# Other positions for projections, convolutions and C in the background of a chunk, and another position for the first shifted copies

## The reference

```
h = layernorm(x) * (1 + ca) + sa
x = x + ga * (concat([mamba_f(h), flip(mamba_b(flip(h)))]) @ wproj.T + bproj)
h = layernorm(x) * (1 + cb) + sb
x = x + gb * (quantized(h) @ quantized(weight).T + bias)

mamba(x):                                   # 1024 channels d, 16 states n
    u, z = split(x @ win.T)
    u = silu(causal conv of u over 4 time steps + bconv)
    dt, B, C = split(u @ wx.T)              # 32, 16 and 16 columns
    delta = softplus(dt @ wdt.T + bdt)
    h[t,d,n] = exp(delta[t,d] * A[d,n]) * h[t-1,d,n] + delta[t,d] * u[t,d] * B[t,n]
    y = sum over n of h[t,d,n] * C[t,n] + u * Dp
    return (y * silu(z)) @ wout.T
```

## Time and profile before

| | |
|---|---|
| median of three runs | 7735.96 us |
| profiled execution, its own time | 7733.82 us |
| its span, first to last instruction | 7731.9 us |
| mean granted clock of PE | 0.969 of full speed |
| scan stage (first to last scan) | 233 to 7307 us |
| DVE, POOL, PE, ACT busy | 92%, 90%, 89%, 79% of the span |
| SP's transfers | 1038.78 MB in the main queue |

### The profile page before, as it was taken

One profiled execution on the slowest core, in us unless ns is written; L12 is line 12 of the kernel. 1 busy time (PEld: TensorE's weight loads), 2 busy tenths in 40 slices (PEclk: granted clock), 3 DMA queues, 4 the chain that ended last, 5 costly groups with the idle time before them and its releaser, 6 DMA issues. The chain is left out here.

```text
span 7731.9 us, 140320 instructions
## 1 busy us (share of the span) xinstructions
PE 6883.3 (89%) x32680; PEld 4030.1 (52%) x32680; DVE 7095.4 (92%) x11547; ACT 6125.9 (79%) x11641; POOL 6970.5 (90%) x3806
## 2 busy tenths in 40 slices
PE   6899888999898889999888898999888998888889
PEld 3455555555555555555555555555555555555445
DVE  1799999999999999999999999999999999999766
ACT  1788888888888888888888888888888888888745
POOL 0899999999999999999999999999999999999768
PEclk8999999999999999999999999999999999999989
DMA  5444445444444553444445434444454354444555
GB/s 163 143 134 127 129 141 146 105 139 136 128 129 127 146 147 101 143 133 134 126 125 148 146 101 141 131 132 132 125 146 145 103 144 129 132 130 127 144 200 171
DMA packets 597340, 1049.44 MB, mean 136 GB/s; under 512 B 113456, under 2 KB 221872, under 8 KB 588016
## 3 DMA queue, kind: packets, MB, share of 16 engines
q1 hardware_dynamic: 594384, 1038.78, 45.7%
q10 hardware_dynamic: 2080, 1.05, 0.0%
HBM read 909.69 MB, written 129.91 MB: 134 GB/s over the span
## 5 line engine op out<-in xcount | busy, mean ns | idle before, releaser
L618 POOL TENSOR_TENSOR dBu<-Bb,du 128x1024 f32<-128x1024 f32 x2048 | 4794.8, 2364 | 30.5 <-DVE h L1133 22.4
L748 ACT ACTIVATE dA<-delta,A 128x512 f32<-128x512 f32 x4096 | 2777.8, 694 | 553.6 <-DVE hR L1133 232.7
L1133 DVE TENSOR_TENSOR_SCAN h<-dA,state,dBu 128x512 f32<-128x512 f32 x1792 | 2309.3, 1289 | 326.7 <-ACT dA L748 256.2
L969 PE MATMUL yT<-ident,hC 128*128 128x128 f32 x9216 | 1431.0, 284 | 400.8 <-DVE hC L1149 384.8
L627 POOL TENSOR_TENSOR hR<-hR,Cb 128x512 f32<-128x512 f32 x1024 | 1301.4, 1271 | 360.7 <-DVE state L1163 360.7
L969 PEld LDWEIGHTS yT<-ident,hC 128*128 128x128 f32 x9216 | 1064.1, 144 | 767.0 <-DVE hC L1149 601.2
L1133 DVE TENSOR_TENSOR_SCAN hR<-dA,state,dBu 128x512 f32<-128x512 f32 x1024 | 1291.9, 1262 | 9.0 <-ACT dA L748 9.0
L1149 DVE TENSOR_TENSOR hC<-h,Cb 128x512 f32<-128x512 f32 x1792 | 1214.0, 677 | 0.0
L962 PE MATMUL bg<-u,comb 128*128 128x512 f32 x2112 | 989.2, 594 | 0.9 <-DVE u L1091 0.9
L923 PE MATMUL bg<-hT,win_z 128*128 128x512 f32 x2048 | 966.6, 594 | 19.0 <-ACT sp_a L644 19.0
L1133 DVE TENSOR_TENSOR_SCAN hV<-dA,state,dBu 128x512 f32<-128x512 f32 x768 | 966.2, 1258 | 3.5 <-PE bg L916 2.6
(11 more groups left out here) (159 smaller groups left out, 8479.2 us busy)
## 6 DMA issues: line engine op xcount, KB each, us to landing
comb<-pre_scratch SPq DMA_DIRECT2D x1040, 256.0 KB, 4.7
Bb<-bc_scratch SPq DMA_DIRECT2D x264, 512.0 KB, 8.4
Cb<-bc_scratch SPq DMA_DIRECT2D x264, 512.0 KB, 7.6
win_u<-in_win SPq DMA_DIRECT2D x264, 256.0 KB, 4.6
pre_scratch<-pre SPq DMA_DIRECT2D x264, 256.0 KB, 3.6
comb<-comb_scratch SPq DMA_DIRECT2D x66, 1024.0 KB, 7.3
win_z<-in_win SPq DMA_DIRECT2D x257, 256.0 KB, 2.7
part_scratch<-pre SPq DMA_DIRECT2D x132, 256.0 KB, 2.0
```

What stands on the lines that cost most here:

```text
L618: pool.tensor_tensor(dBu[:, q % AHEAD], Bb[:, 2 * q:2 * q + 2, :], du[:, j % 2, :].unsqueeze(1).broadcast_to([P, 2, T]), ALU.mult).then_in ...
L748: act.activation(dA[dA_bank(v, j, n)][:], delta[:, j % 2, :], ACT.Exp, scale=A[:, v % 2, j * N + n:j * N + n + 1]).then_inc(dA_made, 1)
L969: ins = nc.tensor.matmul(yT[:, tt * P:(tt + 1) * P], product[:, tt * P:(tt + 1) * P], ident[:], start=first and tt == 0, stop=False, is_tr ...
L1133: nc.vector.tensor_tensor_scan(to, dA[dA_bank(v, j, n)][:], dBu[:, q % AHEAD, k, :], state[:, c:c + 1], ALU.mult, ALU.add).then_inc(h_made, 1)
```

## The change

Nine units get another position or bank, K is taken one position later, and the copies for C0 are loaded at position 20 (`FIRST_TAPPED`), where they were loaded right behind the store of U0 at position 22.

| unit | positions, bank before | after | taken by ACT before, after |
|---|---|---|---|
| U0 | 20, 20, bank 1 | 17, 17, bank 1 | 22, 19 |
| Z2 | 17, 18, bank 1 | 19, 20, bank 1 | 20, 22 |
| Z5 | 40, 41, bank 0 | 41, 42, bank 1 | 43, 44 |
| U6 | 41, 41, bank 1 | 40, 40, bank 0 | 43, 42 |
| C5 | 43, bank 0 | 42, bank 0 | 45, 44 |
| U7 | 43, 43, bank 1 | 44, 44, bank 1 | 45, 46 |
| C6 | 45, bank 0 | 46, bank 0 | 47, 48 |
| C7 | 48, bank 0 | 49, bank 0 | 50, 51 |
| X | 50, 51, 53, 54 | 51, 51, 53, 54 | 56, 56 |
| K | 56, bank 1 | 56, bank 1 | 57, 58 |

```diff
--- before.py
+++ after.py
@@ -65,12 +65,12 @@
 GENERAL = [
     ("D1", (0,), 0), ("Z0", (1, 2), 1), ("O0", (2, 2, 3, 3, 4, 4, 5, 5), 0), ("O1", (6, 6, 7, 7, 9, 9, 10, 10), 0),
     ("D2", (7,), 1), ("Z1", (9, 10), 1), ("O2", (11, 11, 12, 12, 13, 13, 14, 14), 0), ("D3", (15,), 1),
-    ("O3", (15, 15, 17, 17, 18, 18, 19, 19), 0), ("Z2", (17, 18), 1), ("U0", (20, 20), 1), ("U1", (21, 21), 0),
+    ("O3", (15, 15, 17, 17, 18, 18, 19, 19), 0), ("U0", (17, 17), 1), ("Z2", (19, 20), 1), ("U1", (21, 21), 0),
     ("D4", (23,), 1), ("C0", (24,), 0), ("Z3", (25, 26), 1), ("U2", (26, 26), 0), ("C1", (28,), 0),
     ("U3", (28, 29), 1), ("C2", (31,), 0), ("D5", (31,), 1), ("U4", (33, 33), 0), ("Z4", (33, 34), 1), ("C3", (35,), 0),
-    ("U5", (36, 36), 1), ("C4", (38,), 0), ("D6", (39,), 1), ("Z5", (40, 41), 0), ("U6", (41, 41), 1), ("C5", (43,), 0),
-    ("U7", (43, 43), 1), ("C6", (45,), 0), ("D7", (47,), 1), ("C7", (48,), 0), ("Z6", (49, 50), 1),
-    ("X", (50, 51, 53, 54), 0), ("K", (56,), 1), ("D0", (56,), 0), ("Z7", (58, 59), 0), ("H0", (58,), 1),
+    ("U5", (36, 36), 1), ("C4", (38,), 0), ("D6", (39,), 1), ("U6", (40, 40), 0), ("Z5", (41, 42), 1), ("C5", (42,), 0),
+    ("U7", (44, 44), 1), ("C6", (46,), 0), ("D7", (47,), 1), ("C7", (49,), 0), ("Z6", (49, 50), 1),
+    ("X", (51, 51, 53, 54), 0), ("K", (56,), 1), ("D0", (56,), 0), ("Z7", (58, 59), 0), ("H0", (58,), 1),
     ("H1", (60,), 1), ("H2", (61,), 0), ("H3", (62,), 1),
 ]
 OWN_BANK = 2
@@ -92,7 +92,7 @@
 
 
 MIDWAY = [f"Z{j}" for j in range(MT)] + [f"T{j * N + TURNED[-1]}" for j in range(MT)]
-TAKE = {name: at[-1] + (2 if name[0] in "ZTUCDX" else 1) for name, at, bank in SCHEDULE}
+TAKE = {name: at[-1] + (2 if name[0] in "ZTUCDXK" else 1) for name, at, bank in SCHEDULE}
 assert all(TAKE[name] <= POS - 1 for name in TAKE)
 BY_ACT = [name for name in sorted(AT, key=lambda name: (TAKE[name], name not in MIDWAY, NUM[name])) if name[0] != "Y"]
 EVA = len(BY_ACT)
@@ -360,6 +360,9 @@
         kept = lambda g, q: g * len(KEEPING) + len([k for k in KEEPING if k < q])
 
 
+        FIRST_TAPPED = max(TAKE["U0"], AT["O3"][-1] + 1)
+
+
         IN_PLACE = [n for n in STRAIGHT if n % 2]
         dA_bank = lambda v, j, n: (n + v * MT + j) % 3
 
@@ -468,8 +471,9 @@
 
                                 sp.wait_ge(hist_stored, i * 16 + 48)
                                 sp.dma_start(A[:, 1 - s], dram["A"][:, d1, :]).then_inc(A_loaded[1 - s], 16)
-                                sp.wait_ge(pre_stored[0], i * 64 + 80)
-                                load_tapped(1 - s, 0)
+                    if p == FIRST_TAPPED:
+                        sp.wait_ge(pre_stored[0], i * 64 + 80)
+                        load_tapped(1 - s, 0)
                     if p == TAKE["U7"] + 1:
                         sp.wait_ge(hist_made, i * MT + 2 * MT + 1)
                         store_hist(s)
```

## The result

The changed kernel takes 7762.4 us (median of 6 runs, 7760.5 to 7768.7); the kernel before took 7733.1 in the 6 runs now known of it. The ratio is 1.0039, 95% interval 1.0028 to 1.0049: slower by about 29 us, where I forecast 6 us less.

The account below looks back on a forecast made before the run. DVE sets the end and loses time only where ACT brings a `dA` late; -10.8 + 18.2 - 8.6 - 1.5 - 3.5 = -6.2 us, from a median of 7736.0 to 7730 us, forecast range 7720 to 7743 (0.57).

Parts of the forecast that it names:

- C6, C7, K: Later takes by ACT: C6 -10.8 us at 48.0, C7 +18.2 at 53.0, K -8.6 at 58.0.
- The -1.5 at 60: Position 60: five small delays that follow from K's stalls at 58.0 go, -1.5 us.
- the 0.53: Before position 51's second `dA`: ACT's wait of 0.53 us for a scan stays.
- A new wait of X for the bank of C7: Sign on PE: X, first pieces at 51, must wait for C7's bank, some 1.1 us of PE.
- ACT's wait of about 1 us: Sign at 58: ACT waits about 1 us or less for K, behind D0's take.
- U6, Z5, C5, U7: Positions 40 to 44: half of the 4.7 us of stalls at 44.0 goes, and 0.08 in some 20 others, -3.5 us.
- my signs of being wrong: 24.0 loses its wait, 43.0 or 20.0 gains one, or positions that no edit touches change their times.
- C0's copies: First shifted copies loaded at 20 instead of 22: PE alone could gain, 0 us.
- C6's copies: PE's wait for them, 2.94 us in the fifteenth chunk, goes; nothing added to the sum.
- U0 and Z2: Positions 17 to 20: PE's stretch stays full, U1 ready at 3403.1 both times, 0 us; bounds -24.6 and some +3.
- Rival 2: ACT from 51.1 to 53.0: only C7 counts, price 18.2 us, slower, about 7750; chance 0.13.
- rival 1: PE was the thing at 24 (U1 earlier), or its clock: -20 to -30 us, about 7710; chance 0.22.

Follow-up runs that it names:

- experiment 8: Kernel before with only C6 at 46 instead of 45, its take at 48 instead of 47: 7718.2 us, ratio 0.9985.
- experiment 6: Kernel before with only C7 at 49 and X at 51, 51, 53, 54: 7753.7 us, ratio 1.0037.
- experiment 7: Kernel before with only K's take one position later: 7724.4 us, ratio 0.9999.
- experiment 4: Changed kernel with the load of the first shifted copies back at position 22: 7764.5 us, ratio 1.0051.
- experiment 1: Changed kernel with PE doing U0 ahead of the turned state at position 17: 7729.5 us, ratio 0.9998.
- experiment 2: Kernel before with only the turned state drawn ahead of Z2's first part within position 17: 7776.3 us, ratio 1.0063.
- Experiment 9: Changed kernel with U0 ahead of the turned state at 17, C7 and X back in old positions, U1 from 21 to 22: 7689.3 us, ratio 0.9953.

## Why the prediction was wrong

*C6, C7, K.* Right in mechanism and, at their positions, in size: -10.8, +18.0 and -8.6 against -10.8, +18.2 and -8.6, each shown alone in experiments 8, 6 and 7. The -1.5 at 60 came out too, but by luck: it shows in every trace, with K moved or not. Of the run's time experiment 7 doesn't show the 8.6. ACT's rows around the `dA` of 53.0 after, in the fifteenth chunk: the second `dA` of 51, which waits for its scan, then C7's take where the forecast put it, and the `dA` of 53.0:

```profile
3508.88 0.69 ACT L752 ACTIVATE dA<-delta,A 128x512 f32<-128x512 f32 x1 [0.92 <-DVE hR L1137]
...
3510.51 0.70 ACT L675 ACTIVATE u<-bg,bconv 128x512 f32<-128x512 f32 x1
...
3518.53 1.30 ACT L752 ACTIVATE dA<-delta,A 128x512 f32<-128x512 f32 x2
```

In front of that `dA` ACT waits 0.92; the forecast had the 0.53 stay. The difference is idle time ahead of the full stretch and costs nothing. A new wait of X for the bank of C7, which I had forecast, isn't in the table after. K is there before ACT comes; ACT's wait of about 1 us is now for D0, where the forecast had it for K, behind D0's take:

```profile
3536.10 0.69 ACT L647 ACTIVATE sp_r<-bg,bdt 128x512 f32<-128x512 f32 x1 [1.02 <-PE bg L955]
...
3537.25 0.21 ACT L699 COPY CT<-bg 128x64 f32<-128x64 f32 x1
```

*U6, Z5, C5, U7.* -1.1 instead of -3.5 (a slip stands in the term: half of 4.7 and 20 x 0.08 make 3.9). All four stalls of 44.0 are gone and 0.08 at 43 in 22 chunks, 6.7 us. I left out what the wait for U6 costs when PE comes to position 40 late: 43.0 now stalls in five chunks, by 0.36 to 1.00, which was one of my signs of being wrong. No experiment has these units alone, but the traces fall in two kinds. In the six with U6 in its old place 43.0 never stalls and 44.0 does in 1 to 5 chunks; in the six with the new place it is the reverse, 43.0 in 1 to 6 chunks and 44.0 never. Positions 41 to 44 together are 2.8 us shorter in the second kind on average, with 7 us between the traces of one kind, so the term was about right and its size in one trace is chance. In the clean fifteenth chunk ACT waits 1.62 us for U6 (forecast 1.4). In the twenty-sixth PE works at half clock after a wait for copies (clock 0.50 from 5916 to 5920; L955 takes 2.07 us, not 1.12). ACT waits for PE's `yT`, which stalls 41.1 by 1.21 before U6 plays a part (before has such a stall in its twentieth chunk); then U6 holds ACT, and 43.0 stalls by 1.00:

```profile
5911.92 1.07 PE L920 MATMUL bg<-comb,wtap 128*32 128x512 f32 x8 [2.33 <-DMA comb<-pre_scratch]
...
5915.42 2.07 PE L955 MATMUL bg<-dbc,wdt 32*128 32x512 f32 x2
...
5926.37 0.26 ACT L670 ACTIVATE hist<-bg,cur 128x3 f32<-128x3 f32 x1 [1.97 <-PE bg L905]
...
5927.82 1.29 DVE L1137 TENSOR_TENSOR_SCAN h<-dA,state,dBu 128x512 f32<-128x512 f32 x1 [1.00 <-ACT dA L752]
```

*C0's copies.* Right: 0, shown by experiment 4. *C6's copies.* Right: PE's wait is gone (100.8 us in 32 waits before, none after), and positions 45 and 46 are as long as before.

*U0 and Z2.* This step failed: "An exchange inside a full stretch doesn't bring its last unit forward: U1 is ready at 3403.1 both times." The first half holds, the second doesn't follow. I had summed the durations of PE's rows and taken "busy in every moment" for "waits for nothing". But the order in the queue had hidden a wait, and the exchange took the cover away: I wrote down what I thought each part of the change would uncover for ACT, and never asked which of PE's own instructions stood behind the piece that I moved, and for whom they wait. The number was to be had. The gate of before ends at 3387.07, O3's piece at about 3386.3, so without Z2's piece the turned state waits 0.8 us; times 32, at a place where a stall of 0.7 says that ACT passes on every delay, that is 25 us and more. The table of waits of before even had the wait, 56 times, at other tiles. What the runs showed in place of the 0: PE's wait at 17, 0.94 us lost in each chunk, U1 1.0 us later and +31.2 us at position 23, taken away by experiment 1 and made by experiment 2 in the kernel before. Of my bounds for this step the upper, +3, had no row behind it; that is why the range missed.

*The rivals.* The forecast of the sign failed with this step. Rival 2 named a slower case of about this size, with the wrong place: its C7 is a part (+18.0), but the other gains did come. Of rival 1 the premise didn't come true, U1 came later and not earlier, but its link did: 24.0 follows PE's U1 one to one, here the wrong way round. Its clock brought nothing. Experiment 9 shows that the stall of 24.0 goes once U1's take, with ACT's wait for U1, no longer stands ahead of the gate.

## What to carry to other kernels

A queue that is busy without a gap may still be full of waits that just don't show: before you move a unit, look at what moves up into its place, which semaphore that instruction waits for, and when it is set. Then sum the stretch again. And a stall of a few tenths in each turn marks a place where every further delay counts in full, and every gain until the stall is used up (C6's take left with 0.68 us and gave back 0.34 a chunk): of all work on the late engine ask whether it has to stand ahead of that point (here two normalizations and one take with its wait did not: 44.6 and 24.6 us at their positions).

## What the runs showed of the hardware

A gap on PE costs more than the brackets say. A piece of O3 with work behind it takes 1.72 us from its start to the next start, but its row says 1.88; at position 17 the gap of 0.78 is counted from the end of these 1.88, and the loss is 0.94 us.

PE's clock gave nothing back. The waits for copies fell from 176.8 to 70.3 us, and the mean granted clock is 0.968, where it was 0.969. PE's waits for DVE's `hC` rose in the same trace (453.5 us on L973 after, 384.8 us on L969 before), and so did those for `u` above; PE is idle for 866.5 us of the span after and for 848.6 before. The Trainium skill ("TensorE: Matmul & The Clock Gate", HAM oscillation) has it that work behind a wait for transfers is paid at half rate. The twenty-sixth chunk above agrees (0.50 behind a wait of 2.33 us); that fewer such waits return time over the whole run, as I had drawn from it for rival 1, no run here shows.
